# A vision-transformer block on one core: the exponentials of the activation engine without a bias tile, and one more addition on the vector engine

## The reference, cut to what matters

```python
h = concat([cls, patches(x) @ W.T + b])                  # 4 images, 3137 tokens, 128 features
y = layernorm(h)
q, k, v = y @ Wq, y @ Wk, y @ Wv                         # 8 heads of 16 features
attn = softmax(einsum('bhsd,bhtd->bhst', q, k) * 16 ** -0.5 + pos_bias)
h = h + (attn @ v) @ Wo
h = h + ffn(layernorm(h))                                # token pooling, gate, 2 of 8 experts, exact gelu
```

## Time and profile before

| | us |
|---|---|
| median of three executions | 3053.28 |
| the profiled execution | 3047.63 |
| its span, first to last instruction | 3045.9 |
| ACT busy | 2700.9 (89%) |
| PE busy | 2662.4 (87%) |
| DVE busy | 1618.8 (53%) |
| POOL busy | 873.9 (29%) |
| ACT busy in line 900 alone, 2167 instructions | 2382.5 |

### The profile page before, as it was taken

One profiled execution on the slowest core, in us unless ns is written; L12 is line 12 of the kernel. 1 busy time (PEld: TensorE's weight loads), 2 busy tenths in 40 slices (PEclk: granted clock), 3 DMA queues, 4 the chain that ended last, 5 costly groups with the idle time before them and its releaser, 6 DMA issues.

```text
span 3045.9 us, 123842 instructions
## 1 busy us (share of the span) xinstructions
PE 2662.4 (87%) x55860; PEld 1235.2 (41%) x55860; DVE 1618.8 (53%) x2543; ACT 2700.9 (89%) x2733; POOL 873.9 (29%) x1424
## 2 busy tenths in 40 slices
PE   7988888888888888888889888888888888999897
PEld 3443333333343333333334333333433333455454
DVE  5744666666656556545565565455655654344410
ACT  4679999999999999999999999999999999734453
POOL 2223333333333333333333333333333323100000
PEclk9989999999999999999999999999999999999999
DMA  5540000000101100011010000110100000300010
GB/s 142 168 142 23 29 28 30 28 27 27 38 27 33 30 30 27 27 48 36 30 33 30 30 27 28 48 37 28 33 30 30 27 28 29 117 22 30 13 34 20
DMA packets 65912, 125.43 MB, mean 41 GB/s; under 512 B 10035, under 2 KB 55181, under 8 KB 63893
## 3 DMA queue, kind: packets, MB, share of 16 engines
q1 hardware_dynamic: 63324, 110.93, 11.5%
q0 software_dynamic: 2048, 6.43, 0.6%
HBM read 67.30 MB, written 51.30 MB: 39 GB/s over the span
## 4 chain that ended last, share of the span: by engine, by line
ACT 48%; PE 22%; issue 21%; DVE 5%; DMA 3%; SPq 0%; POOL 0%; ACTq 0%; DVEq 0%; POOLq 0%
ACT shared L900 47%; PE ps L775 5%; PE ps L783 5%; PE ps L814 5%; PE ps L732 3%; PE ps L759 2%; DMA k_halves<-halves 2%; PE ps L729 1%; DVE root L1091 1%; DVE std L1023 1%; PE ps L671 1%; DVE root L1134 0%; DVE root L1136 0%; DVE root L1084 0%; DVE root L1082 0%
## 5 line engine op out<-in xcount | busy, mean ns | idle before, releaser
L900 ACT ACTIVATE shared<-ps,lift_t 128x1179 f32<-128x1179 f32 (+1 forms) x2167 | 2382.5, 1281 | 35.0 <-PE ps L732 25.9
L814 PE MATMUL ps<-shared,va 64*32 64x393 f32 x25600 | 1596.2, 508 | 0.8 <-issue 0.4
L983 POOL TENSOR_TENSOR shared<-shared,e_all 128x310 f32<-128x310 f32 (+19 forms) x1344 | 815.7, 621 | 1618.4 <-ACT shared L900 1606.5
L732 PE MATMUL ps<-qa,ka 48*32 48x393 f16 (+2 forms) x15200 | 737.5, 324 | 160.1 <-ACT shared L900 150.5
L729 PE MATMUL ps<-qa,ka 51*32 51x393 f16 (+8 forms) x13184 | 652.1, 315 | 144.3 <-ACT shared L900 139.7
L814 PEld LDWEIGHTS ps<-shared,va 64*32 64x32 f32 x25600 | 606.9, 139 | 40.3 <-issue 5.9
L732 PEld LDWEIGHTS ps<-qa,ka 48*32 48x32 f16 x15200 | 241.4, 92 | 688.4 <-ACT shared L900 650.9
L729 PEld LDWEIGHTS ps<-qa,ka 51*32 51x32 f16 x13184 | 207.6, 90 | 740.6 <-ACT shared L900 726.5
L1061 DVE COPY xc<-ps 128x393 f32<-128x393 f32 x64 | 36.4, 569 | 617.3 <-PE ps L814 617.3
L1091 DVE SCALAR_TENSOR_TENSOR root<-root 128x393 f32<-128x393 f32 x486 | 318.9, 656 | 16.7
L919 ACT ACTIVATE qa<-ps,b 128x393 f32<-128x393 f32 x256 | 136.6, 586 | 108.4 <-PE ps L775 108.4
(11 more groups left out here) (150 smaller groups left out, 1640.8 us busy)
## 6 DMA issues: line engine op xcount, KB each, us to landing
qa<-q_halves SPq DMA_DIRECT2D x64, 196.5 KB
ka<-k_halves SPq DMA_DIRECT2D x64, 196.5 KB
att_rows<-std SPq DMA_DIRECT2D x64, 196.5 KB, 3.4
v_rows<-v_sb SPq DMA_DIRECT2D x4, 1600.0 KB, 6.8
va<-v_rows SPq DMA_DIRECT2D x32, 200.0 KB, 15.9
ln_rows<-ln SPq DMA_DIRECT2D x32, 196.5 KB, 5.5
q_halves<-halves SPq DMA_DIRECT2D x32, 196.5 KB, 3.0
k_halves<-halves SPq DMA_DIRECT2D x32, 196.5 KB, 4.0
```

Source lines behind the costliest of these rows:

```text
L732: last = nc.tensor.matmul(out[x:y, cut:W], ka[r:r + 48, par, k0 + x:k0 + y], qa[r:r + 48, par, q0 + cut:q0 + W], start=True, stop=True, ti ...
L814: last = nc.tensor.matmul(ps[quad:quad + 32, O_PS + half, 0:W], va[r:r + 64, par, :, kt], pr[r:r + 64, g % SLOTS_PR, j], start=(kt == 0), ...
L900: nc.scalar.activation(pr[:, g % SLOTS_PR, 0:m], ps[:, b0:b0 + m, 0:W], ACT.Exp, bias=lift_t[:, 0:1], scale=-1.0 / (LOG2E * LIFT * LIFT)). ...
L983: nc.gpsimd.tensor_tensor(p, p, e_all[0:keys, n % HEADS, t:t + z - a], ALU.mult).then_inc(s_biased, 1)
```

## The change

It takes the bias tile away. ACT's exponential at line 900 is called without `bias`, and so with the default of zero. DVE's first step adds a second constant, `EXP2_OFFSET`, ahead of the rounding constant, in the same instruction. This moves the interval over which the fraction runs, and the polynomial's coefficients are fitted to the moved interval such that the leading one is again left out, now without the extra factor. The tile, its memset, its semaphore and ACT's one wait for it go.

```diff
-EXP2 = (8.683946354612057e+20, 1.4695436761694208e+17, 12433933467648.0, 701432768.0, 29850.568359375)
-EXP_LIFT = 0.386022442659754
+EXP2 = (5.902953881462406e+20, 9.989570803479347e+16, 8447052480512.0, 481097408.0, 18444.99609375)
+EXP2_OFFSET = 2281.1142578125
...
-        lift_t = sbuf(top, "lift_t", [P, 1])
...
-            s_lift = semaphore(held, "f_lift")
...
                 nc.scalar.activation(e_all[:], e_all[:], ACT.Exp).then_inc(s_e, 1)
-                act.wait_ge(s_lift, 1)
                 for g in range(NG):
...
                     nc.scalar.activation(pr[:, g % SLOTS_PR, 0:m], ps[:, b0:b0 + m, 0:W],
-                                         ACT.Exp, bias=lift_t[:, 0:1], scale=-1.0 / (LOG2E * LIFT * LIFT)).then_inc(s_exp, 1)
+                                         ACT.Exp, scale=-1.0 / (LOG2E * LIFT * LIFT)).then_inc(s_exp, 1)
...
-                nc.vector.memset(lift_t[:], EXP_LIFT).then_inc(s_lift, 1)
                 dve.wait_ge(s_load, 16 * 9)
...
-                    nc.vector.tensor_scalar(whole, score, ROUND, None, ALU.add).then_inc(s_d_step, 1)
+                    nc.vector.tensor_scalar(whole, score, EXP2_OFFSET, ROUND, ALU.add, ALU.add).then_inc(s_d_step, 1)
```

## The result

| | before | after |
|---|---|---|
| median of four executions each, us | 3050.89 | 2873.54 |
| the profiled execution, us | 3047.63 | 2869.71 |
| its span, us | 3045.9 | 2868.0 |

The ratio is 0.9425, with a 95% interval of 0.9398 to 0.9451. The kernel is 177 us faster; the prediction had the median at 2903 us in a range of 2863 to 2965. All ratios here compare executions in the faster of the chip's two states; one execution of the kernel before, beside the last three experiments, was in the slower one (3233 us, granted clock 0.75) and is not in them.

The account below looks back on a forecast made before the run. The prediction took ACT's exponentials to bound the attention. Its terms, 147 + 0 + 0 + 0 - 12 + 12 = 147 us, gave a median of about 2903 us, range 2863 to 2965.

Parts of the forecast that it names:

- Item 1: ACT's full-group exponentials at line 900 without bias tile: 0.080 us saved on each of 1838, gain 147 us (51 to 197).
- the three near values: Savings per exponential on ACT: line 900 against L862 0.079, against L856 0.067, L919 pair against L862 0.094 us.
- the 67 places that I left out: Exponentials at line 900 before which ACT stood visibly idle; taken off the 1905 full groups, leaving 1838 that gain.
- Rival A: ACT's tile costs what the L919 pair and the cast say, 0.094 to 0.107 us: 2856 to 2880 us; 20%.
- The sum's last line: Whole kernel: 147 us off the profiled 3047.63 gives 2901; with the median 5.6 us higher, about 2903 us.
- C: On ACT, the bias fetch is already hidden, or the call without bias reads a zero tile: 3053 us; 6%.
- B: PE becomes the bound in turns with a batch, which win only half: 2967 us (2930 to 3035); 21%.
- Item 2: The 261 groups of 786 columns: the next scores come last, so cheaper ACT gains 0 (21 us if it did).
- Item 3: DVE's first step, L1082: the second addition costs 0; even another pass of some 0.4 us would fit the slack.
- Item 4: At the start, the memset, the semaphore and one wait go; DVE waits for the weights anyway: 0 us.
- Items 5 and 6: In the attention: lateness of PE and DVE at about 60 places, -12 us; a third fewer low-clock dips, +12 us.
- D: Slower clock in turns without a batch: 1.3 us a dip, 113 further dips take the time past 3053 us; 3%.

Follow-up runs that it names:

- the last three experiments: Scores of two units made twice in 469 turns, on the kernel before (0.9943) and after (0.9460); third shared group in 45 passes on the kernel after (0.9695).
- the clock experiment: The kernel before, with PE making the scores of two units twice in 469 turns without batch or guest: 3032.06 us, ratio 0.9943.

## Why the prediction was right, and where its size was off

**The bound.** Right. ACT set the pace in the attention, and what came off its instruction came off the end.

**Item 1, the tile.** The mechanism was right, the term too small: 147 us instead of 177. This term makes the 30 us between forecast and result. 24 of them come from the price, 0.080 us instead of 0.093, and 6 from the 67 places that I left out: the distances after all 1905 full groups add up to 2192.6 us before and 2013.2 after, 179 less, so that nothing was lost there in sum. Of the 13 ns, about 6 are rounding. The unrounded starts of the trace before have medians of 0.389 us after L862, 0.722 after L856 (my 0.73), 0.487 in the L919 pair and 1.127 after a full group; with them the three near values are 0.083, 0.078 and 0.098, 0.086 on average. The other 7 come from comparing different instructions. The fixed part after the change is 1.034 - 0.982 = 0.052 us, below that of L862 (0.062) and L856 (0.067), the unbiased activations that I took for it. What makes it smaller isn't shown; both are followed by a copy or a cast, line 897 by its own kind. The pair of equal size, L919 against L862, had given 0.094, and I averaged it with two worse ones. The Trainium skill (ScalarE: Activation LUTs, section "What ACT_TABLE_LOAD costs") has about 93 ns for such an operand; the traces agree, with 0.091 to 0.093. The overlap of neighbours, though, is 0.177 us without the tile and 1.320 - 1.134 = 0.186 us with it, not the 93 ns that the prediction quotes beside it, and the measurement decides. The reading by which the fetch hides behind the instruction ahead is excluded by the result itself, and by the scale tile's run. Rival A, which had 2856 to 2880, describes the outcome better than the forecast's own range of 2880 to 2930, in which the result does not lie.

**The sum's last line.** It does not come out as written: 3047.63 - 147 is 2901, and a median 5.6 us above the profiled execution would be 2906, not 2903. Rivals A and C start from 3053, B from about 3050. These 3 us decide nothing.

**Item 2, the short groups.** Right to 2 us. The 261 distances sum to 233 us before and 235 after. In the example of the earlier trace rows the short group started at 627.586 by the unrounded record and the next exponential 0.899 us later. In the trace after, the same group and its follower are 0.885 apart:

```profile
589.43 0.98 ACT L897 ACTIVATE shared<-ps 128x786 f32<-128x786 f32 x1
...
590.32 2.20 ACT L897 ACTIVATE shared<-ps 128x1179 f32<-128x1179 f32 x2
```

ACT alone would need some 0.71: that is the distance in the one place after where the scores behind a short group were early.

**Item 3, DVE's second addition.** Right: 567 ns, and a ratio of 1.0006 for this half by itself.

**Item 4, the start.** Right as far as one can see. The attention's first exponential starts at 205.24 us for 208.35, and what follows the last one is 2.8 us longer; in the seven experiments, which leave both stages alone, the first lies between 206.8 and 212.0 and the second between 413 and 417.

**Items 5 and 6, lateness and the clock.** They cancelled, as forecast, but each was as large as I put it or larger. The time at the low clock, in stretches that began in the attention, fell from 82 to 20 us, three quarters and not one third; at the 0.24 us of the clock experiment that is 15 us back, at my price of 1.3 us for 3.4 us it would be 24. Against it stands lateness. Beyond ACT's own pace (1.127 and 1.034 us), the distances after full groups hold 46 us before and 43 after, though the clock has given its part back; so an estimated 12 to 21 us of new lateness came in. 117 exponentials now follow late scores after a full group, for 72.

**The rivals.** B had PE becoming the bound. It has not, but it is near: the scores were early by 0.33 us in the median before and by 0.23 after, and an estimated 0.2 us more work in 469 turns of PE cost 10 us after, where it had gained 15 to 17 before. C fell with the first row of line 897. D fell too: the low clock receded. PE's idle time in a turn without a batch went with ACT's pace, 0.71 us with two tiles, 0.62 with one and 0.53 with none, and the stretches of low clock that began in the attention went with it, 49, 23 and 5.

**The signs named beforehand.** A distance of 1.04 to 1.05 us (1.034 to 1.043), a mean duration near 1.24 (1.22), ACT's idle time below 60 us (34.1), L1082 unchanged, the last stage unchanged, a clock of 0.98 or more (0.99): all came but for the size of the first two.

## What to carry to other kernels

When an engine is the bound and runs thousands of instructions, its operands are worth counting: here a 128 x 1 bias tile cost ACT 0.09 us per instruction, filled with zeros as much as with a constant, at 786 columns as much as at 1179, and a scale tile beside it the same again. A constant bias may be folded into a free place (here a second addition in a DVE instruction, which takes 567 ns with one and with two), or a factor common to all can be left out where it cancels. To price an operand, compare instructions of equal size and kind with and without it, by the distance between starts; and look beforehand for the groups where the engine is not what comes last, as they give nothing back.

## What the runs showed of the hardware that was not expected

- Operands read from a 128 x 1 tile add up on ACT: 1.043, 1.134 and 1.226 us from start to start for none, one and two, with 1179 columns from PSUM to SBUF. Neighbouring instructions overlap by 0.18 to 0.21 us and hide little of it: a tile lengthens the instruction itself by 0.100 us (1.220 to 1.320) and the distance by 0.091.
- A kernel got faster by repeating work: 469 turns with eight or more further matmuls each brought the time at 1.2 GHz, in stretches that began in the attention, from 82 to 27 us and the ratio to 0.9943.
- Short idle times of PE brought the clock down as well as long ones: 20 of 23 stretches at 1.2 GHz followed idle times of at most 0.63 us each. In the kernel after, with 0.53 us in such turns, none did, and all 5 followed a single stall of 1.2 us or more. That is no threshold: with the third shared group one stretch came at 0.53 us too.
- One more shared group in 45 of 64 passes cost 82 us, with DVE busy for only 67% of the stage. The loss sits at the new groups, 24 of which found DVE in the middle of a guest's steps; the mean load said nothing of that.
